# Two cross-attention layers, order within a step: transposes of the step's own chunk first, key and value projections between the maxima

## What is computed

```python
x = x + _L0_xattn_ref(_layernorm(x), ctx_1024, Wq, Wk, Wv, Wo, bo)            # 8 heads of 64
...
x = x + _L1_xattn_ref(_layernorm(x), ctx_1024, ctx_1024, wq, bq, wk, bk, ...)  # 16 heads of 16, with biases

def _L0_xattn_ref(x, context, Wq, Wk, Wv, Wo, bo):
    ...
    scores = jnp.einsum('bhnd,bhmd->bhnm', q, k) * scale
    attn = jax.nn.softmax(scores, axis=-1)
    out = jnp.einsum('bhnm,bhmd->bhnd', attn, v)
    ...
    return out @ Wo + bo
```

## Time and profile before

| | |
|---|---|
| median of 3 runs | 1932.38 us (1929.84 to 1934.37) |
| profiled execution, own time | 1927.47 us |
| its span | 1925.5 us |
| mean granted TensorE clock | 0.913 |
| instructions in the span | 26912 |
| 8-head cross-attention, about | 30 to 620 us of the span |
| 16-head cross-attention, about | 1040 to 1735 us of the span |

### The profile page before, as it was taken

The page is one execution under the profiler, slowest core; times in us unless marked ns, Lnnn a source line. Parts: engine busy times, 40 slices in busy tenths (PEclk is TensorE's granted clock), DMA queues, the critical chain, the costliest instruction groups (busy, mean ns, idle before and its releaser), DMA issues. The chain is left out here.

```text
span 1925.5 us, 26912 instructions
## 1 busy us (share of the span) xinstructions
PE 1664.0 (86%) x10311; PEld 1208.0 (63%) x10311; DVE 1117.2 (58%) x1880; ACT 793.3 (41%) x1084; POOL 499.8 (26%) x630
## 2 busy tenths in 40 slices
PE   5889999999999668779997888999999899885289
PEld 3667777777777467568886555555566555342278
DVE  4766666666653465356654777776756777106651
ACT  3435554554544132224442111555556455661110
POOL 0003433433469000000000200443433434640000
PEclk9989999999999877679998777899999999997589
DMA  2112221222222100022230110111001010000243
GB/s 77 44 44 67 66 61 50 67 67 58 53 60 52 33 1 1 23 88 87 87 98 11 33 32 27 31 34 34 23 23 34 23 34 12 2 1 22 88 156 117
DMA packets 75443, 92.35 MB, mean 48 GB/s; under 512 B 7442, under 2 KB 62276, under 8 KB 75332
## 3 DMA queue, kind: packets, MB, share of 16 engines
q1 hardware_dynamic: 75140, 90.79, 15.8%
q10 hardware_dynamic: 192, 0.05, 0.0%
HBM read 73.47 MB, written 0.52 MB: 38 GB/s over the span
## 5 line engine op out<-in xcount | busy, mean ns | idle before, releaser
L571 POOL CAST st<-ef 32x512 fp32r<-32x512 f32 x384 | 233.0, 607 | 397.9 <-PE score L1136 354.4
L1676 DVE TENSOR_REDUCE mx<-bank 128x1 f32<-128x512 f32 x512 | 311.8, 679 | 42.2 <-PE bank L1148 41.6
L757 ACT ACTIVATE P<-score 128x1024 f32<-128x1024 f32 x256 | 255.9, 1025 | 129.1 <-PE score L1136 128.8
L1148 PE MATMUL bank<-ef,qm 128*128 128x512 f32 x512 | 234.4, 505 | 41.3 <-DVE mx L1676 21.4
L948 PE MATMUL bank<-c_hi,w_split 128*128 128x512 f32 x640 | 233.1, 425 | 23.7 <-DVE c_lo L1542 8.4
L1148 PEld LDWEIGHTS bank<-ef,qm 128*128 128x128 f32 x512 | 105.9, 207 | 154.9 <-DVE mx L1676 107.4
L1136 PE MATMUL score<-qs,st 97*128 97x512 f32 x512 | 173.3, 426 | 12.9 <-ACT P L757 8.7
L948 PEld LDWEIGHTS bank<-c_hi,w_split 128*128 128x128 f32 x640 | 128.7, 201 | 78.1 <-issue 39.8
L1567 DVE TENSOR_REDUCE mx<-bank 128x1 f32<-128x512 f32 x256 | 162.3, 682 | 22.1 <-PE bank L993 13.6
L536 POOL TENSOR_TENSOR sum<-sum,P 128x512 f32<-128x512 f32 x84 | 111.2, 1324 | 210.0 <-ACT P L673 210.0
L673 ACT ACTIVATE P<-score 128x1024 f32<-128x1024 f32 x128 | 129.9, 1024 | 78.5 <-PE score L982 76.0
(11 more groups left out here) (315 smaller groups left out, 2646.0 us busy)
## 6 DMA issues: line engine op xcount, KB each, us to landing
c_in<-in_ctx SPq DMA_DIRECT2D x64, 512.0 KB, 4.0
w<-k SPq DMA_DIRECT2D x128, 128.0 KB, 2.2
arena<-in_L_ffn_w SPq DMA_DIRECT2D x16, 1024.0 KB, 5.2
arena<-in_L_ffn_W SPq DMA_DIRECT2D x16, 1024.0 KB, 5.4
x<-in_x SPq DMA_DIRECT2D x1, 512.0 KB, 3.7
raw<-in_L_xattn_Wk SPq DMA_DIRECT2D x1, 512.0 KB, 6.4
raw<-in_L_xattn_Wv SPq DMA_DIRECT2D x1, 512.0 KB, 7.3
raw<-in_L_xattn_Wq SPq DMA_DIRECT2D x1, 512.0 KB, 8.1
```

The costliest lines, as they stand in the source:

```text
L571: pool.tensor_copy(st1[32 * block:32 * block + 32, k, :], ef1[rows, g % LAG, part, :].bitcast(F32)).then_inc(a[f"st{k}"], 16)
L757: act.activation(P1[:, index % PRING, :], score[n % 2][:], ACT.Exp).then_inc(a["p"], 1)
L1148: mm(dst[:], qm1[:, h, 128 * q:128 * q + 128], ef1[:, g % LAG, 0, :], start=True, stop=True).then_inc(a["ms"], 1)
L1676: v.tensor_reduce(mx1[:, u % 2, i, n:n + 1], ring[n % 3][:], AX.X, ALU.max).then_inc(a["red"], 1)
```

## The change

Both layers get new lists. The transposes of a step's own chunk come first in the step, not those of the next chunk at its end. In `cross0` k0 comes after the maxima of head 1, between m3 and m4; k1, v0 and v1 stay after mixture 0 and mixture 1. In `cross1`, in steps with t % 8 != 0, mixture 1 of the chunk before and then k0 come after m3, v0 after m5, v1 after m9; in steps with t % 8 == 0 keys, mixture 1 and values stay at the end. The ring is counted through these lists, so uses get other predecessors. ScalarE and VectorE get lists to match. The keys of `cross1` get a tenth buffer, and some tensors other addresses for it. The same work is done, with the same instructions.

```diff
+ERING = LAG + 1
...
-        ef1 = at("ef1", 0, [LAG, 2, CHUNK], F32R)
+        ef1 = at("ef1", 0, [ERING, 2, CHUNK], F32R)
...
+        order0 = ["d", "t0", "t1", "m0", "m1", "m2", "m3", "k0", "m4", "m5", "m6", "m7", "k1", "v0", "v1"]
+        even1 = ["t0", "t1", "m0", "m1", "m2", "m3", "k0", "m4", "m5", "v0", "m6", "m7", "m8", "m9", "v1", "m10", "m11", "m12", "m13", "m14", "m15"]
+        last1 = ["t0", "t1", *(f"m{n}" for n in range(16)), "k0", "v0", "v1"]
...
+        def order_of1(t):
+            return even1 if t % NCH else last1
...
+        def bank_of(a, t, use):
+            return ring[order0.index(use) % 3] if a is a0 else ring[(order_of1(t).index(use) + 1) % 3]
+
+        def freed(a, t, use):
+            order, used = (order0, use0) if a is a0 else (order_of1(t), use1)
+            place = order.index(use) - 3
+            while True:
+                if place < 0:
+                    t -= 1
+                    if t < 0:
+                        return None
+                    order = order0 if a is a0 else order_of1(t)
+                    place += len(order)
+                before_it = used(t, order[place])
+                if before_it:
+                    return before_it
+                place -= 3
...
@@ ScalarE, cross0
+                    if 0 < t < CHUNKS:
+                        for f in range(2):
+                            context_high(a, c_hi0, t, f)
+                    for h in range(HPU0):
+                        if g >= 0:
                             weights(g, h)
+                        if h == 2 and t < CHUNKS:
+                            keys(t, 0)
                     if t < CHUNKS:
-                        for n in range(2):
-                            keys(t, n)
+                        keys(t, 1)
...
-                    if t + 1 < CHUNKS:
-                        for f in range(2):
-                            context_high(a, c_hi0, 13 + f, t + 1, f)
@@ ScalarE, cross1
+                    for n in range(8):
+                        if g >= 0:
+                            if n == 1 and g and g % NCH == 0:
+                                sums(g // NCH - 1)
                             weights(g, n)
+                        if i and t < CHUNKS:
+                            if n == 2:
+                                keys(t)
+                            if n in (3, 5) and u % 2 == 0:
+                                values(u, i, n // 2 - 1)
@@ TensorE, cross0
+                    if 0 < t < CHUNKS:
+                        turn(a, t, 0)
+                        turn(a, t, 1)
                     for h in range(HPU0):
                         if g >= 0:
                             scores(g, h)
                         if 1 <= t <= CHUNKS:
                             maxima(t - 1, h)
+                        if h == 1 and t < CHUNKS:
+                            keys(t, 0)
                     if g >= 0:
                         mixture(g, 0)
                     if t < CHUNKS:
-                        keys(t, 0)
                         keys(t, 1)
...
-                    if t + 1 < CHUNKS:
-                        turn(a, freed0, 13, t + 1, 0)
-                        turn(a, freed0, 13, t + 1, 1)
@@ TensorE, cross1
+                        if n == 1:
+                            if g > 0 and g % NCH:
+                                mixture(g - 1, 1)
+                            if t < CHUNKS and not at_end:
+                                keys(t)
+                        if n in (2, 4) and t < CHUNKS and not at_end and u % 2 == 0:
+                            values(t, n // 2 - 1)
                         if g >= 0 and n == 5:
                             mixture(g, 0)
...
+                    if at_end:
+                        if t < CHUNKS:
+                            keys(t)
+                        if g >= 0:
+                            mixture(g, 1)
...
@@ VectorE, cross0
+                    if 0 < t < CHUNKS:
+                        context_of(t)
+                    for h in range(HPU0):
+                        if 1 <= t <= CHUNKS:
                             reduce(t - 1, h)
+                        if h == 2 and t < CHUNKS:
+                            low_keys(t, 0)
...
@@ VectorE, cross1
+                    if 0 < t < CHUNKS:
+                        for f in range(2):
+                            context_low(a, c_hi, c_lo, t, f)
+                    for h in range(HPU1):
+                        if 1 <= t <= CHUNKS:
                             reduce(t - 1, h)
+                        if i and h == 2 and t < CHUNKS:
+                            low_keys(t)
...
                     if g > 0 and g % NCH == 0:
                         finish(g // NCH - 1)
-                    if t + 1 < CHUNKS:
-                        for f in range(2):
-                            context_low(a, c_hi, c_lo, 19, t + 1, f)
```

More of the change, by code:

```diff
@@ L198, in values1, with use1 @@
         def values1(u, i):
             return 2 * (NCH * (u // 2) + i)
[L202 to L207, removed]
-                return None
[L209 to L216, removed]
-            return freed1(t, place)
+        def use1(t, use):
+            kind, n = use[0], int(use[1:])
+            if kind == "m":
+                return ("red", 16 * (t - 1) + n + 1) if 1 <= t <= CHUNKS else None
+            if not 0 <= t < CHUNKS:
+                return None
+            if kind == "v":
+                return ("v", values1(t // NCH, t % NCH) + n + 1) if t // NCH % 2 == 0 else None
+            return ("kl", t + 1) if kind == "k" else ("cl", 2 * t + n + 1)
@@ L675, in keys @@
                 def keys(g, n):
-                    src = ring[(9 + n) % 3]
+                    src = bank_of(a, g, f"k{n}")
                     act.wait_ge(a["kp"], a.n("kp", 2 * g + n + 1))
@@ L726, in cross0 @@
                     if t < CHUNKS:
-                        for n in range(2):
-                            values(t, n)
-                    if t + 1 < CHUNKS:
-                        for f in range(2):
-                            context_high(a, c_hi0, 13 + f, t + 1, f)
+                        values(t, 0)
+                        values(t, 1)
                     if t % NCH in (2, 3, 4, 5) and t // NCH + 1 < UNITS:
@@ L745, in weights1 @@
                 for f in range(2):
-                    context_high(a1, c_hi, 19 + f, 0, f)
+                    context_high(a1, c_hi, 0, f)
             def cross1():
@@ L761, in keys @@
                     act.wait_ge(a["kp"], a.n("kp", g + 1))
-                    act.activation(ef1[:, g % LAG, 0, :], ring[16 % 3][:], ACT.Identity, bias=bias[:, 2 + half:3 + half]).then_inc(a["kh"], 1)
+                    act.activation(ef1[:, g % ERING, 0, :], bank_of(a, g, "k0")[:], ACT.Identity, bias=bias[:, 2 + half:3 + half]).then_inc(a["kh"], 1)
                 def values(u, i, n):
@@ L936, in turn, with place_free @@
                 last.then_inc(a["tr"], 1)
-            def place_free(a, freed, t, place):
-                before_it = freed(t, place)
+            def place_free(a, t, use):
+                before_it = freed(a, t, use)
                 if before_it:
                     pe.wait_ge(a[before_it[0]], a.n(*before_it))
-                return ring[place % 3]
+                return bank_of(a, t, use)
             def three(dst, pairs):
@@ L1686, in low_keys @@
                     dve.wait_ge(a["kh"], a.n("kh", g + 1))
-                    v.scalar_tensor_tensor(out=ef1[:, g % LAG, 1, :], in0=ring[16 % 3][:], scalar=bias[:, 2 + half:3 + half],
-                                           in1=ef1[:, g % LAG, 0, :].bitcast(F32), op0=ALU.add, op1=ALU.subtract).then_inc(a["kl"], 1)
+                    v.scalar_tensor_tensor(out=ef1[:, g % ERING, 1, :], in0=bank_of(a, g, "k0")[:], scalar=bias[:, 2 + half:3 + half],
+                                           in1=ef1[:, g % ERING, 0, :].bitcast(F32), op0=ALU.add, op1=ALU.subtract).then_inc(a["kl"], 1)
                 def finish(u):
@@ L1700, in cross1 @@
                 for f in range(2):
-                    context_low(a, c_hi, c_lo, 19, 0, f)
+                    context_low(a, c_hi, c_lo, 0, f)
                 dve.wait_ge(set1["bias"], 16 * 21)
```

166 lines of the change are left out of this document (69 added, 97 removed).

## The result

After 2096.24 us (median of 4, 2093.86 to 2102.25), before 1931.11 (median of 4, 1928.92 to 1934.37): ratio 1.086, 95% interval 1.083 to 1.089. The forecast case held (2070, range 2000 to 2110). The profiled span is 2094.0 against 1925.5: **+168.5 us** for the same instructions, where +138 was foreseen.

What follows compares the result with a forecast made beforehand. TensorE was taken as busiest, with waits in the three-bank ring deciding. Terms 60 + 29 + 16 + 0 + 14 + 24 + 7 - 12 = +138 on the profiled 1927.5 gave 2065, with the runs' median 4.9 above: 2070, range 2000 to 2110.

Steps and rivals of the forecast that it cites:

- The forecast case: Whole kernel: the new order's ring waits and clock falls cost time, total 2035 to 2100 around 2070; chance 0.62.
- 8-head full steps: 8-head layer, t = 9 to 31: +2.5 us in each of 23 steps, 0.4 more in eight with query copies, +60.
- m6 stall: 8-head full steps: m6 takes k0's bank, so TensorE stands 2.5 us a step waiting for the key subtractions.
- The clock: 8-head full steps: the 2.5 us gap brings the half level in 0.85 of 23 steps, 1.5 us each, +29.
- 8-head filling: 8-head layer, t = 1 to 8: 13.7 us a step at full clock against 12.5, plus clock falls, +16.
- The context load: Start of a step: load issued there, not at the previous step's end, but wanted a whole step later; 0.
- 16-head layer, full: 16-head full steps: +14 in 14 without values, +24 in seven with values, +7 for the division; +45.
- draining: 16-head draining: late mixture comes after two further scores, steps fall from 10.5 to 8.8 us; seven steps, -12.
- (1): Rival, whole kernel: stalls come but the clock stays up, 2026 us; chance 0.2.
- (2): Rival, 8-head full steps: half level comes twice in most, after the m6 stall and at step start, 2105 us; chance 0.1.
- (3): Rival, both layers: mixed work wins, each step falls to its busiest engine's work, 16-head filling 12.6, total 1803 us; chance 0.04.
- (4): Rival: m6 stall is there, but the 16-head layer gains 3 to 4 us in 28 steps, 1948 to 1920; chance 0.04.

Runs made afterwards that it cites:

- the filler: Changed kernel plus 36 matmuls of zeros between head 3's scores and m6 in 19 full 8-head steps: 2073.37 us, against 2096 without.
- the finer mixtures: Kernel before with VectorE's query subtractions ahead of the key subtraction (1921.56), plus each 16-head step's two mixtures cut into eight pieces: 1936.0 us.

## Why the prediction was right, and where it was not

**The method** held: going through the new lists place by place and asking who is three places earlier. 8-head full steps: +60 for 23 steps, that is 57 for 22; the filler shows 57. The parts were less exact, and that they sum so well has some luck in it: a plain step took 2.35 more where 2.5 was foreseen, one with query copies 3.1 where it was 2.9. The working of the m6 stall gave 2.5, the trace shows 2.2 to 2.3; t1 waits 0.25 for v1's copy, not 0.45; and the wait for c_lo, priced as removed, is 5.0 us in ten steps, before 5.9 in twenty.

**The clock** was foreseen at 0.85 of the steps times 1.5 us. It fell in 13 of 22 steps, 16 falls in all, at 1.4 to 1.6 each: 24 instead of 28. The count of steps was too high. The Trainium skill, TensorE: Matmul & The Clock Gate, section A second HAM failure mode: psum-queue depth-cycling, describes a bf16 kernel whose clock goes up and down because TensorE idles briefly between groups of matmuls as it cycles through PSUM banks. The filler's trace agrees, with 1.00 in all the steps whose idle time is filled.

**8-head filling** (t = 2 to 8: +14 foreseen, +17.5 found) was near in sum and not in its parts: 13.7 at full clock, as worked out, in t = 2 and 7, but 17.0 with two stretches at the half level in t = 3 to 6.

**Failed: the start.** "The context load ... is wanted a whole step later" looked at the load alone. At t = 1 the transposes are now behind the layer's query projections and the parts of the context behind that again, which the projections covered before: m1 waits 3.5 us for c_lo, and m6 2.7 for k0. TensorE's waits after, 0 to 60 us:

```profile
PE bank L1015 <- DVE c_lo L1572: 3.7, 2, 3.5
PE bank L1015 <- DVE k L1609: 2.7, 1, 2.7
```

The clock adds to it: 0.83 at t = 1, before 1.00. Priced at 2 as one of the eight filling steps, it is +8.0 in the first layer; in the second, priced at 0, it is +1.7, although m1 waits 4.3 us for c_lo there, since before a maximum waited 4.1 us for a reduction. The walk through the lists took the steady step and left out t = 0 and 1, which have other work in them.

**16-head layer, full**: +45 foreseen with the divisions, +37.8 found. The division's wait is 6.3 us where 5.3 of work was foreseen; t = 18 takes 29.3. This is the timeline, VectorE and then TensorE:

```profile
1491.76 3.34 DVE L1585 RECIPROCAL den<-den 128x512 f32<-128x512 f32 x1
...
1498.23 1.29 DVE L1572 TENSOR_TENSOR c_lo<-bank,c_hi 128x512 fp32r<-128x512 f32 x2
...
1498.97 0.80 PE L1171 MATMUL bank<-ef,qm 128*128 128x512 f32 x1 [6.32 <-DVE c_lo L1572]
```

Against that t = 9 got shorter (16.7 instead of 19.4): its second mixture moved into t = 10, and its clock was 0.90 where it had been 0.82. This was not in the sum. The wait of v0 for k0's subtraction (L1687 of before, L1718 now) was foreseen at 2.3 and m8's for v0's copy at 0.85. TensorE's waits in the values steps, 1469 to 1632 us:

```profile
PE bank L970 <- DVE ef L1718: 14.1, 7, 2.0
PE bank L1171 <- DVE c_lo L1572: 11.2, 7, 6.3
PE bank L1171 <- ACT v L784: 2.7, 4, 0.7
```

2.0 in each of seven steps, and 0.7 in four.

**Failed: draining, -12.** A draining step takes 10.55 us, before 10.43. ScalarE's list after:

```profile
1847.09 3.85 ACT L774 ACTIVATE P<-score 128x1024 f32<-128x1024 f32 x4 [1.43 <-PE score L1159]
1852.37 3.84 ACT L774 ACTIVATE P<-score 128x1024 f32<-128x1024 f32 x4 [1.43 <-PE score L1159]
1857.64 2.93 ACT L774 ACTIVATE P<-score 128x1024 f32<-128x1024 f32 x3 [1.43 <-PE score L1159]
```

Twice a step ScalarE stands for 1.43, as it does before:

```profile
1653.66 5.69 ACT L757 ACTIVATE P<-score 128x1024 f32<-128x1024 f32 x6 [1.38 <-PE score L1136]
1660.79 1.94 ACT L757 ACTIVATE P<-score 128x1024 f32<-128x1024 f32 x2 [1.43 <-PE score L1136]
```

A mixture takes TensorE 1.85 us, the scores have two banks, so ScalarE has at most two exponentials left to do when it begins and is dry before the next scores: 8 x 0.96 + 2 x 1.43 = 10.5 in either order. Foreseen were "ScalarE's 7.7 plus two short gaps"; the gap's size doesn't depend on whose mixture it is. Of the last row of the table (+8.9) the seven draining steps are 0.8. The largest other part is t = 32, with 2.8: there the first scores of the last unit wait 2.45 us for the load of their shift (L1159 for DMA qs), which before was 0.61.

**The rivals.** (1) and (2) fell: the falls are neither none nor two in most steps. The total came out 30 us above the forecast: about 21 in the last row of the table, 13 of it the draining, 8 from t = 31 of the 8-head layer to the 16-head layer, mostly the clock, 8 at the two starts, and 5 in filling, against 7 less in the 16-head full steps and 4 less in the 8-head ones. (3) fell: 16-head filling took 17.2, not 12.6, and even the finer mixtures lost 14 us to the same kernel without them (1936.0 against 1921.56). (4) fell: the 16-head full steps lost 38 us and gained nothing.

## What to carry to other kernels

Before reordering uses of a small ring of banks, write the new order down and name for each use the one that held its bank; if that one is read out by a chain over several engines, add up the chain, with what stands ahead of it in each queue, and compare it with what the waiting engine has in between. Do this for the first steps and the steps with extra work too. And look in such a change for the part that pays by itself: here it was query work ahead of the reductions and a division ahead of c_lo on VectorE, worth 17 us without touching TensorE's order.

## What the hardware showed unasked

- Going from the other matmuls to those of the narrow tile (128*17) and back costs about 0.3 us, so a block of them is cheaper in one piece.
- Products of zeros are enough to keep the clock at 1.00 through a stall of 2.3 us; in t = 9 to 30 of the 8-head layer this gave 18 us.
- Falls of the clock scatter: the same 752 matmuls between the layers took 223.8 us in one kernel and 231.0 in another (0.72 and 0.69). Why the one kernel and not the other, no run shows.
